# A two-layer graph convolution whose adjacency tiles become the stationary operand, with new layouts of the one-hot factors

## What is computed

```python
def gcn_conv(x, W, b, src, dst, n):
    h = x @ W
    s = jnp.concatenate([src, loops]); d = jnp.concatenate([dst, loops])
    deg = segment_sum(ones, d)                       # 200000 edges and 6250 self-loops
    norm = rsqrt(deg)[s] * rsqrt(deg)[d]
    return segment_sum(h[s] * norm[:, None], d) + b
g = relu(gcn_conv(service_emb, W1, b1, src, dst, 6250))   # rows of 32 features
g = gcn_conv(g, W2, b2, src, dst, 6250)
x = concatenate([user_emb[user_idx], g[context_idx].reshape(512, 96)], axis=1)
return x @ fc_W + fc_b                               # (512, 128) @ (128, 6250)
```

## Time and profile before

| | |
|---|---|
| median of 3 runs | 1049.21 us (1047.53 to 1050.67) |
| profiled execution: its time, its span | 1050.32 us, 1048.2 us |
| PE busy | 778.9 us |
| DVE busy | 783.0 us |
| ACT busy | 565.4 us |
| moved by DMA | 90.67 MB |

### The profile page before, as it was taken

One profiled execution on the slowest core, in us unless ns is written; L12 is line 12 of the kernel. 1 busy time (PEld: TensorE's weight loads), 2 busy tenths in 40 slices (PEclk: granted clock), 3 DMA queues, 4 the chain that ended last, 5 costly groups with the idle time before them and its releaser, 6 DMA issues.

```text
span 1048.2 us, 18364 instructions
## 1 busy us (share of the span) xinstructions
PE 778.9 (74%) x7657; PEld 568.2 (54%) x7657; DVE 783.0 (75%) x1196; ACT 565.4 (54%) x1211; POOL 172.6 (16%) x122
## 2 busy tenths in 40 slices
PE   0170658785949389721489899999999999999688
PEld 0150546563736267511467777777777656666433
DVE  9999497997695997897899999999999410000066
ACT  0390559775848288600378888898889900000000
POOL 0000000002000000004744545455520000000220
PEclk9965666555555555555699999999999999999899
DMA  4000000000000000002131434333330087756167
GB/s 94 1 2 0 1 1 2 1 2 4 1 1 1 1 2 2 1 0 56 34 144 53 175 113 159 129 144 144 144 135 1 6 363 290 300 193 251 15 212 282
DMA packets 32148, 90.67 MB, mean 87 GB/s; under 512 B 19357, under 2 KB 21277, under 8 KB 29502
## 3 DMA queue, kind: packets, MB, share of 16 engines
q1 hardware_dynamic: 21790, 81.16, 20.2%
q0 software_dynamic: 3648, 6.69, 3.0%
q10 hardware_dynamic: 6624, 1.60, 0.7%
HBM read 45.28 MB, written 44.16 MB: 85 GB/s over the span
## 4 chain that ended last, share of the span: by engine, by line
DVE 57%; PE 31%; issue 7%; ACT 3%; DMA 2%; POOL 0%; DVEq 0%; ACTq 0%
DVE arena L874 14%; PE pp L1178 12%; DVE arena L730 11%; DVE arena L729 8%; PE pp L1056 4%; DVE arena L863 4%; PE psY L1040 4%; PE pp L1231 3%; DVE arena L700 2%; PE psY L1041 2%; DVE arena L832 2%; PE pp L1100 2%; DVE arena L703 2%; DVE arena L718 1%; ACT arena L566 1%
## 5 line engine op out<-in xcount | busy, mean ns | idle before, releaser
L566 ACT ACTIVATE arena<-pp 128x1024 fp8e4<-128x1024 f32 x307 | 283.1, 1052 | 89.6 <-PE pp L1100 89.1
L525 ACT ACTIVATE arena<-iota_lo,arena 128x128 fp8e4<-128x128 f32 x785 | 231.5, 393 | 77.8 <-PE psY L1040 46.8
L1100 PE MATMUL pp<-arena 128*128 128x128 fp8e4 x2401 | 190.2, 224 | 39.9 <-DVE arena L874 39.0
L1100 PEld LDWEIGHTS pp<-arena 128*128 128x128 fp8e4 x2401 | 165.4, 102 | 94.8 <-issue 44.5
L486 POOL DMA_INDIRECT arena<-ordered_keys,window x98 | 155.0, 1581 | 364.5 <-DVE parts L820 228.4
L1041 PE MATMUL psY<-arena 128*128 128x49 fp8e4 x1563 | 214.3, 213 | 0.0
L1037 PE MATMUL psY<-arena 128*128 128x49 fp8e4 x778 | 161.7, 214 | 69.2 <-DVE arena L718 69.2
L1113 PE MATMUL psY<-arena,parts 128*96 128x512 fp8e4 (+1 forms) x637 | 182.0, 375 | 0.5 <-ACT y_s L554 0.5
L1040 PE MATMUL psY<-arena 128*128 128x49 fp8e4 x785 | 167.0, 218 | 17.3 <-ACT arena L525 15.2
L874 DVE TENSOR_TENSOR arena<-arena 128x3072 int32<-128x3072 bf16 (+3 forms) x52 | 165.6, 3229 | 0.1
L1041 PEld LDWEIGHTS psY<-arena 128*128 128x128 fp8e4 x1563 | 148.3, 115 | 0.5
(11 more groups left out here) (179 smaller groups left out, 690.8 us busy)
## 6 DMA issues: line engine op xcount, KB each, us to landing
adjacency_spill<-arena SPq DMA_DIRECT2D x9, 3136.0 KB, 10.8
arena<-adjacency_spill SPq DMA_DIRECT2D x9, 3136.0 KB, 11.2
out_dram<-arena SPq DMA_DIRECT2D x48, 256.0 KB, 2.3
arena<-in_L_rec_fc_W_dram SPq DMA_DIRECT2D x1, 3125.0 KB, 11.3
arena<-in_L_rec_fc_b_dram SPq DMA_DIRECT2D x1, 3125.0 KB, 10.9
arena<-ordered_keys,window POOLq DMA_INDIRECT x98, 3.0
adjacency_spill<-arena SPq DMA_DIRECT2D x1, 784.0 KB, 4.6
arena<-adjacency_spill SPq DMA_DIRECT2D x1, 784.0 KB, 4.4
```

The lines of the kernel that those rows point to most:

```text
L525: nc.scalar.activation(step_lo[:, s % LORING, :], iota_half[:], ACT.Sign, bias=neg_lo[:, c:c + 1], saturate=False).then_inc(lo_ready, 1)
L566: nc.scalar.activation(adj8[g % SLOTS][:, n0 * P:n1 * P], pp[gp % 3][:, 0:(n1 - n0) * P], ACT.Copy, saturate=False).then_inc(evicted, 1)
L1100: ins = MM(pp[gp % 3][:, (n - n0) * P:(n - n0 + 1) * P], oh8[h][0][:, n - a, :], oh8[h][1][:, n - a, :], start=True, stop=True)
```

## The change

- Aggregation in both layers: the adjacency tile (128x128 fp8) is the stationary operand and the 96 feature columns stream (`spread`), so sums have nodes on partitions. The three parts are summed by a reduction on DVE.
- W1 is applied to the embeddings at the start, with blocks of the weights on a diagonal (`W1b`); W2 is applied to the result of layer one (`turn_x`, `copy_x`, `linear_x`), and layer two ends with the reduction, scale and bias.
- `post` is split into `post_sum` (end of the period) and `post_split` (between the masks and the second half of the one-hots).
- `thirds` lies tile by tile, eight values side by side, compared with each tile's code written twice side by side (`c1_16`, `octal`); `quads` lies value by value.
- `masks` writes 16 bits, `pick` is bf16. Fetches wait for the masks and for a pair count (`PACE`) that spreads them over a period.
- Output: six PSUM banks, four buffers of 1024 or 1130 columns, stores from the queues of SP and ACT in turn.

```diff
+MRING = 8
+PACE = (-14, -8, -2, 4)
...
-        thirds = at(o, 8 * 2 * NT * 2, BF16).rearrange("p (w n) -> p w n", w=8)
+        thirds = at(o, 8 * 2 * NT * 2, BF16).rearrange("p (n w) -> p n w", w=8)
...
-        quads = at(o, 4 * 2 * NT * 2, BF16).rearrange("p (n v) -> p n v", v=4)
+        quads = at(o, 4 * 2 * NT * 2, BF16).rearrange("p (v n) -> p v n", v=4)
...
-        res = at(E0, 4 * BANK * 4, F32).rearrange("p (k n) -> p k n", k=4)
...
+        OUT_W = [2 * BANK] * 5 + [N - 10 * BANK]
+        OUT_AT = [sum(OUT_W[:k]) for k in range(len(OUT_W))]
+        RES_B = max(OUT_W) * 4
+        res = at(E0, 4 * RES_B, F32).rearrange("p (k n) -> p k n", k=4)
...
+        bank = lambda n: pp[n % 6 // 2][:, n % 2 * BANK:(n % 2 + 1) * BANK]
+        psT = psX[:, 200:200 + P]
+        psZ = psX[:, 336:336 + P]
...
+        def write_out(eng, mine):
+            out_v = out.rearrange("(p b) n -> p b n", b=BB)
+            for n in range(mine, BB * len(OUT_W), 2):
+                b, j = divmod(n, len(OUT_W))
+                eng.wait_ge(fc_read, b * len(NCH) + sum(1 for c, w in NCH if c < OUT_AT[j] + OUT_W[j]))
+                eng.dma_start(out_v[:, b, OUT_AT[j]:OUT_AT[j] + OUT_W[j]], res[:, n % 4, 0:OUT_W[j]]).then_inc(stored[n % 4], 16)
...
+            sp.wait_ge(blocks_zero, 1)
+            for k in range(GC):
+                sp.dma_start(W1b[k * D:(k + 1) * D, k * D:(k + 1) * D], W1).then_inc(weights_in, 16)
+                sp.dma_start(W2b[k * D:(k + 1) * D, k * D:(k + 1) * D], W2).then_inc(weights_in, 16)
...
-                        pool.wait_ge(picked, n - RD + 1)
+                        pool.wait_ge(masked, n - RD + 1)
+                    if g >= 2 and pairs_before(g - 2) + PACE[dd] > 0:
+                        pool.wait_ge(filled, pairs_before(g - 2) + PACE[dd])
...
+            for r in range(4):
...
+                act.wait_ge(w1_turned, r + 1)
+                nc.scalar.copy(X_T[:, 0:w * P], pp[2][:, 0:w * P]).then_inc(w1_copied, 1)
+                act.wait_ge(w1_done, r + 1)
+                nc.scalar.copy(X0[:, 4 * GC * r:4 * GC * r + c // D, :].rearrange("p h f -> p (h f)"), pp[2][:, BANK:BANK + c]).then_inc(w1_set, 1)
...
-                w = chunks_of(g) * P
-                nc.scalar.copy(y_s[:, g % 2, 0:w], psY[0:D3, 0:w]).then_inc(y_set, 1)
+                    act.wait_ge(x_set, g - 1)
+                w = chunks_of(g) * D3
+                nc.scalar.copy(y_s[:, g % 2, 0:w], psY[:, 0:w]).then_inc(y_set, 1)
+            def copy_x(g):
+                act.wait_ge(x_turned, g + 1)
+                if g:
+                    act.wait_ge(z_done, g)
...
-                    act.wait_ge(y2_done, i + 1)
...
-                    w = chunks_of(g) * P
-                    nc.scalar.copy(y_s[:, i % 2, 0:w], pp[i % 3][0:D3, 0:w]).then_inc(y2_set, 1)
-                    if i >= 2:
-                        write_table(i - 2, ORDER[i - 2])
-                for i in range(NG - 2, NG):
-                    write_table(i, ORDER[i])
...
-                V.tensor_scalar(tile, tile, low_key[:, d:d + 1], key_step[:, d:d + 1], ALU.subtract, ALU.mult).then_inc(masked, 1)
+                if n >= MRING:
+                    dve.wait_ge(picked, n - MRING + 1)
+                V.tensor_scalar(mk16[:, n % MRING, :, :].rearrange("p q t -> p (q t)"), tile, low_key[:, d:d + 1], key_step[:, d:d + 1],
+                                ALU.subtract, ALU.mult).then_inc(masked, 1)
...
-                V.tensor_copy(c1_16[:, 0, 0:nt], c1_i[:, 0, 0:nt])
-                V.tensor_scalar(c1_16[:, 1, 0:nt], c1_i[:, 1, 0:nt], -8.0, None, ALU.add)
...
+                V.tensor_copy(c1_16[:, :, 0:nt, :], c1_i[:, :, 0:nt].rearrange("p s (n o) -> p s n o", o=1).to_broadcast((P, 2, nt, 2)))
...
-                    V.tensor_tensor(th, io, c1.rearrange("p (o n) -> p o n", o=1).to_broadcast((P, 8, n)), ALU.is_equal)
+                    V.tensor_tensor(th.rearrange("p n (w k) -> p n w k", k=2), io.rearrange("p n (w k) -> p n w k", k=2),
+                                    c1.rearrange("p n (o k) -> p n o k", o=1).to_broadcast((P, n, 4, 2)), ALU.is_equal)
                     for v in range(4):
-                        ins = V.scalar_tensor_tensor(out=qu[:, :, v], in0=c2, scalar=float(v), in1=one.bitcast(F32), op0=ALU.is_equal, op1=ALU.mult)
+                        ins = V.scalar_tensor_tensor(out=qu[:, v, :], in0=c2, scalar=float(v), in1=one.bitcast(F32), op0=ALU.is_equal, op1=ALU.mult)
                 ins.then_inc(made1, 1)
...
-                    ins = V.tensor_tensor(oh32[h][s][:, 0:(b - a) * 32].rearrange("p (n w v) -> p n w v", w=8, v=4),
-                                          thirds[:, :, s * NT + a:s * NT + b].rearrange("p w (n o) -> p n w o", o=1).to_broadcast((P, b - a, 8, 4)),
-                                          quads[:, s * NT + a:s * NT + b, :].rearrange("p n (o v) -> p n o v", o=1).to_broadcast((P, b - a, 8, 4)), ALU.mult)
+                    ins = V.tensor_tensor(oh32[h][s][:, 0:(b - a) * 32].rearrange("p (n v w) -> p n v w", w=8, v=4),
+                                          thirds[:, s * NT + a:s * NT + b, :].rearrange("p n (o w) -> p n o w", o=1).to_broadcast((P, b - a, 4, 8)),
+                                          quads[:, :, s * NT + a:s * NT + b].rearrange("p v (n o) -> p n v o", o=1).to_broadcast((P, b - a, 4, 8)), ALU.mult)
...
+            def thirds_of(y, w):
+                return y[:, 0:w * D3].rearrange("p (h k f) -> p h f k", k=3, f=D)
...
+            def nodes_one(x, g, joined):
                 c, w = first_chunk(g), chunks_of(g)
...
+                joined(V.tensor_tensor(x, x, dis_w(c, w), ALU.mult))
+                joined(V.tensor_tensor(x, x, bias[:, 0:1, :].to_broadcast((P, w, D)), ALU.add))
+                return V.scalar_tensor_tensor(out=x, in0=x, scalar=0.0, in1=dis_w(c, w), op0=ALU.max, op1=ALU.mult)
+            def post_sum(g):
+                w = chunks_of(g)
+                x = xs[:, g % 2, 0:w, :]
+                dve.wait_ge(y_set, g + 1)
+                link(V.tensor_reduce(x, thirds_of(y_s[:, g % 2, :], w), axis=AX.X, op=ALU.add))
+                nodes_one(x, g, link).then_inc(x_set, 1)
+            def split_z(g, joined, x):
+                c, w = first_chunk(g), chunks_of(g)
                 for part in range(2):
-                    joined(V.tensor_copy(parts[1][:, c:c + w, part, :], x))
-                    joined(V.tensor_tensor(x, x, parts[1][:, c:c + w, part, :], ALU.subtract))
+                    joined(V.tensor_copy(parts[1][:, c:c + w, part, :], x if part else z))
+                    joined(V.tensor_tensor(x, x if part else z, parts[1][:, c:c + w, part, :], ALU.subtract))
                 return V.tensor_copy(parts[1][:, c:c + w, 2, :], x)
...
+                if g:
+                    post_split(g - 1)
...
-                post(g)
+                post_sum(g)
...
+                    V.tensor_reduce(x, thirds_of(pp[i % 3], chunks_of(g)), axis=AX.X, op=ALU.add).then_inc(y2_read, 1)
+                    dve.wait_ge(y2_read, i + 1)
+                    to_table(i, g, x, link)
...
+            pe.wait_ge(nodes_in, 32)
+            pe.wait_ge(weights_in, 16 * (2 * GC + 2))
+            for r in range(4):
...
+                for j in mine:
...
+                    ins = nc.tensor.transpose(pp[2][0:w, (j - 4 * r) * P:(j - 4 * r + 1) * P],
+                                              X0[:, j * GC:j * GC + w // D, :].rearrange("p h f -> p (h f)"), ident[:])
+                ins.then_inc(w1_turned, 1)
...
+                    ins = MM(pp[2][:, BANK + (j - 4 * r) * P:BANK + (j - 4 * r) * P + w], X_T[0:w, (j - 4 * r) * P:(j - 4 * r + 1) * P],
+                             W1b[0:w, 0:w], start=True, stop=True)
+                ins.then_inc(w1_done, 1)
...
-                    ins = MM(o, gath[:, n % RD, q, :], same_block[:, 0:NH], start=(q == 0), stop=(q == NQ2 - 1))
+                    ins = MM(o, mkb[:, n % MRING, q, :], same_bf[:], start=(q == 0), stop=(q == NQ2 - 1))
...
-                for b in range(k * PAIR // c, min((k + 1) * PAIR, tiles_of(g)) // c):
-                    MM(psY[0:D3, 0:w], stationary(0, b), adj_view(g % SLOTS, g, b), start=(b == 0), stop=False)
+                for n in range(k * PAIR, min((k + 1) * PAIR, tiles_of(g))):
+                    spread(psY, 0, g % SLOTS, n, c)
+            def spread(tile, layer, slot, n, c):
+                b, dd = divmod(n, c)
+                MM(tile[:, dd * D3:(dd + 1) * D3], adj_tile(slot, n), features(layer, b), start=(n == 0), stop=False)
+            def features(layer, b):
+                return parts[layer][:, b, :, :].rearrange("p k f -> p (k f)")
             def own_rows(tile, layer, g):
                 for dd in range(chunks_of(g)):
-                    ins = MM(tile[0:D3, dd * P:(dd + 1) * P], stationary(layer, first_chunk(g) + dd), identb[:], start=False, stop=(dd == chunks_of(g) - 1))
```

(36 more changed lines are left out.)

211 lines of the change are left out of this document (111 added, 100 removed).

## The result

The kernel after takes 1010.19 us (median of 4 runs, 1009.91 to 1010.95) against 1049.94 of the kernel before on the same chip (1047.53 to 1051.87): a ratio of 0.9624, 95% interval 0.9602 to 0.9645, 3.8% faster. The forecast was 999 with a range of 984 to 1024. The time lies in the range, 11 us above the point. It is also 0.2 us above the 990 to 1010 that the forecast's own chance stood for, where the turn's rival begins (1010 to 1024), so the time alone can't say which of the two came; the stages have to. The profiled execution took 1009.95 us, 1.8 of it around its span of 1008.1.

A forecast was written before the change was run, and what follows sets the result against it. DVE was taken to bound the building stage and PE layer two. Terms -39 - 5.6 - 1.4 + 3.4 - 2.3 - 0.4 - 5 = -50.3 took the profiled 1050.32 us to 1000.0, median 999, range 984 to 1024.

The forecast's parts named there:

- the turn's rival: Building stage: PE reaches its pairs late every period, costing 1 to 2.3 us each; 1010 to 1024 us, chance 0.14.
- Layer two: Layer two: matmuls of 96 columns at 0.042 us make a group 8.5 us instead of 11.62; -39 us.
- the one that calls the reloads hidden: Layer two: reloads are issued early enough to land before needed, the last wide one at 928 against 934; no cost.
- The start: Stretch up to DVE's first mask, when the first gathers have landed: no change, 0 us.
- DVE's period: Building stage: DVE sets the pace, its period falling from 26.62 to 26.1 us; -5.6 us over eleven periods.
- The quads' gain: Building stage, DVE: writing values side by side cuts four quad instructions from 3.46 to 1.87 us; -1.59 per group.
- The turn: Building stage: PE's work queued behind its wait for x_set ends before DVE needs it, hidden by 0.7 us.
- The tail's +3.4: End of layer one: PE starts the last group's pairs later after the last x_set, so the tail grows by 3.4 us.
- Picks and start: From DVE's first mask to group 1: cheaper bf16 picks (-2.3) and shorter fields of group 1 (-1.4); -3.7 us.
- W1 ahead: Kernel start: W1 work fits PE's idle time from 22 to 48 us; cost 0, at most 5 without that cover.
- Output product: Output product: larger SBUF and PSUM rings bridge late stores; -5 us, bounds -8 and -2.
- Weight loads set the pace: Layer two and building: each load must end before the next begins, making the kernel slower; near 1195 us, chance 0.03.

The follow-up runs named there:

- e1: Kernel after, but each of layer two's ten reloads fetches 128 bytes a partition (16 KB) instead of up to 3136 KB: ratio to before 0.9597, layer two 107.9 us.
- e2: Kernel after with full reloads, but one matmul of 384 columns replaces four of 96 in layer two: ratio to before 0.9552, layer two 101.3 us.
- e4: Kernel after with POOL's fill of the table `octal` moved from the start to after the fetches of the user rows: ratio to before 0.9640.
- e9: The kernel before, unchanged, profiled once more on another chip: 1056.14 us (one run).
- e6: Kernel after with the quads laid out as in the kernel before, a tile's four values side by side: ratio to before 0.9833, period 27.98 us.
- e5: Kernel after with turn, copy and W2 product of x after pairs 21, 22 and 24 instead of 13, 14 and 17: ratio to before 0.9601.
- e8: Kernel after with the output product storing single 512-column tiles from a ring of four in SBUF, still six in PSUM: ratio to before 0.9730.
- e3: Kernel after with each 3136 KB reload issued as four transfers of a quarter of the columns: ratio to before 0.9671, layer two 113.8 us.
- e10: Kernel after with each reload of layer two waiting until the one before has landed: ratio to before 0.9724, layer two 109.2 us.

## Why the prediction was right or wrong

- *Layer two, -39 us: right in its mechanism, off by 7.8.* The price of a matmul (0.042 us), of a group (8.5) and of the first group (about 1.4 us over the others) came out. What is missing is a term that the sum does not have: four times as many matmuls mean some four times as many instruction blocks, and seven of the some twenty of layer two were late beside reloads that fill the DMA. The pauses make 7.5 us (from the group times: 113.2 less 12 x 8.50, the small group's 2.25 and the first group's 1.4). The step that failed is the one that calls the reloads hidden: they were hidden as data (no wait for a load stands in the trace), but not as traffic beside PE's instructions. e1 and e2 show it from both sides. In other runs of an unchanged layer two the miss would have been up to 10.6 us (116.0).
- *The start, 0 forecast, +3.5 measured.* The sum left out the new table's fill on POOL. It is priced at 2.8 us (e4); the other 0.7 us arose in the sort, where the kernel before itself varies by as much (end of the splits 483.37, and 484.04 in e9).
- *DVE's period, 26.1: right* (26.2; -6.1 us over the eleven, -5.6 forecast). The quads' gain was sized 1.59 and measured 1.55; e6 confirms its cause. The doubled code's copy is 0.57 us, within the 0.4 to 0.8; the reduction of 0.58 us is the lower of the two values. Mask operations 0.3 us longer, which nothing in the sum had, take back what it saves.
- *The turn: right.* In the period shown x is set at 697.9, PE's last pair for DVE's second half ends at 708.2, 10.3 us later, and DVE asks at 709.2: 1.1 us to spare where 0.7 was forecast. PE waits 3.3 us on average for x_set and DVE hardly ever for PE (1.5 us in all, 1.05 of it in the tail). The rival did not come, though the time alone fits it. The tail's +3.4 was +2.8, and e5 takes it back by placing the turn later.
- *Picks and start: -3.7 forecast, -3.2 measured.*
- *W1 ahead: hidden*, as forecast; PE and ACT were done with it at 38 us, and the first count tile ran at 50.9.
- *Output product, -5: right* in cause (DVE's waits for stores 8.9 us before and 1.7 after; e8). That the size agrees to 0.1 us is partly luck: against the other profile of the kernel before, 51.3 us (e9), the gain is 2.1.
- *Weight loads set the pace:* did not come. Matmuls of 96 columns with a fresh 128x128 load each start 42.5 ns apart, 196 of them in a row; the 81 ns that the Trainium skill, TensorE: Matmul & The Clock Gate, "Back-to-back issue gap", has for pairs of 128 columns are not seen in these.

## What to carry to other kernels

When an edit multiplies the instructions of an engine, count the blocks of 256 that it must fetch, and look whether the DMA is full in that stretch: a stream of weight loads and short matmuls can be bound by neither PE nor its data. A setup instruction on POOL belongs beside DVE operations that it doesn't block, even at the very start. And a transfer that is slowed for the good of one stage has to be followed to where its bytes then land.

## What was not expected of the hardware

- PE's instructions come late under a full DMA: pauses of 0.2 to 1.7 us (the longest in e4 and e8), a block of 256 instructions or several apart, and none in nine groups with the small reloads. Packets of a quarter of the size don't help (e3). The rate alone doesn't say which block is late: from 904 to 914 the DMA moved 341 GB/s and no block was, from 933 to 939 it moved 315 and one was by 1.42 us. What decides which block is late is open.
- On three of four chips PE issued a few matmuls at a time between 503 and 518 us, in both kernels, and lost 7 to 16 us (from DVE's first mask to group 1 the kernels built on after took 27.0 to 35.6 us there, after 19.7 at first; before took 30.2 in e9 and 23.0 at first); left open.
- One POOL fill of 4.05 us stretched a DVE operation of 0.22 us to 2.99, and the same fill beside operations with two operands stretched none.
- One reload of 3136 KB at a time took 11.1 us (nine in 99.8, e10), some 290 GB/s; with two or three in flight the DMA moved 396 to 425 GB/s.
